# A decoder layer on one core: queries join the ring of six units with keys and values, three buffers go, and the order of all steps is written anew

## What is computed

```python
# attention: 16 heads of 16, causal, only the 32 largest scores of a row kept
scores = einsum('bhqd,bhkd->bhqk', q, k) / sqrt(16), causal
attn   = softmax(top-32 of each row of scores, the rest -inf)
y      = (attn @ v) @ Wo.T + bo
x = layernorm(x + y)
# experts: all 8 computed for every token, gated by sums over a context
h = relu(einsum('edi,bsi->bsed', proj_in, x))        # hidden 512
o = einsum('eid,bsed->bsei', proj_out, h)
x = layernorm(x + einsum('bsei,bse->bsi', o, gate))
# feed-forward: Hadamard, 4-bit activations, ternary weights
x = layernorm(x + quantised(x @ H) @ ternary(W).T)
```

## Time and profile before

| what | value |
|---|---|
| median of 3 runs | 575.65 us (575.60 to 576.58) |
| span of the profiled execution | 574.0 us |
| its own time | not listed apart from its span; the median lies 1.65 us above the span |
| TensorE busy | 521.3 us, 91% |
| VectorE busy | 457.4 us, 80% |
| ScalarE busy | 409.2 us, 71% |
| GpSimd busy | 346.6 us, 60% |

### The profile page before, as it was taken

How to read it: one execution, slowest core, us unless ns; L and a number is a source line. 1 busy time by engine, 2 the same in 40 slices (tenths; PEclk the granted TensorE clock), 3 DMA queues, 4 the chain that set the end, 5 groups by cost and what they waited for, 6 DMA issues and landing times. The chain is left out here.

```text
span 574.0 us, 22290 instructions
## 1 busy us (share of the span) xinstructions
PE 521.3 (91%) x8116; PEld 443.4 (77%) x8116; DVE 457.4 (80%) x2846; ACT 409.2 (71%) x1018; POOL 346.6 (60%) x355
## 2 busy tenths in 40 slices
PE   5757659999999999999999999999999999999973
PEld 3535548888888888888888888888888888888851
DVE  2698988896988989998998889998999899504115
ACT  2888788776767687768866687768686878566641
POOL 1587485955547466755574556656565756476762
PEclk9888888999999999999999999999999999999995
DMA  7544440002000101100120102000200010000000
GB/s 228 174 150 148 126 157 18 3 2 59 3 24 18 23 3 38 40 3 21 41 58 2 23 11 67 3 22 3 76 4 22 2 39 3 1 2 19 2 14 24
DMA packets 23230, 24.08 MB, mean 42 GB/s; under 512 B 2129, under 2 KB 20049, under 8 KB 23121
## 3 DMA queue, kind: packets, MB, share of 16 engines
q1 hardware_dynamic: 23120, 22.65, 13.0%
HBM read 18.32 MB, written 2.10 MB: 36 GB/s over the span
## 5 line engine op out<-in xcount | busy, mean ns | idle before, releaser
L541 POOL TENSOR_TENSOR h_lo<-h_raw,h_hi 128x512 f16<-128x512 f32 x128 | 148.9, 1164 | 114.4 <-ACT h_raw L693 113.0
L895 PE MATMUL ps_o<-w_hi,h_lo 128*128 128x256 f16 x512 | 139.7, 273 | 3.5 <-POOL h_lo L541 3.5
L879 PE MATMUL ps_z<-x1t_hi,w_lo 128*128 128x256 f16 x512 | 140.0, 273 | 0.2 <-DVE x1t_lo L1043 0.2
L879 PE MATMUL ps_z<-x1t_lo,w_hi 128*128 128x256 f16 x512 | 139.7, 273 | 0.0
L879 PE MATMUL ps_z<-x1t_hi,w_hi 128*128 128x256 f16 x512 | 139.6, 273 | 0.0
L895 PE MATMUL ps_o<-w_hi,h_hi 128*128 128x256 f16 x512 | 139.6, 273 | 0.0
L895 PE MATMUL ps_o<-w_lo,h_hi 128*128 128x256 f16 x512 | 139.5, 273 | 0.0
L689 ACT ACTIVATE h_hi<-ps_z 128x512 f16<-128x512 f32 x128 | 76.2, 595 | 71.7 <-PE ps_z L879 71.6
L987 DVE MATCH_REPLACE8 taken<-next,taken 128x64 f32<-128x64 f32 (+4 forms) x480 | 110.7, 242 | 0.1
L562 POOL TENSOR_TENSOR acc<-go_sb,acc 128x512 f32<-128x512 f32 x55 | 70.0, 1273 | 34.3 <-ACT go_sb L703 34.2
L982 DVE MAX8 next<-taken 128x8 f32<-128x64 f32 (+4 forms) x480 | 85.5, 245 | 0.1
(11 more groups left out here) (142 smaller groups left out, 1037.3 us busy)
## 6 DMA issues: line engine op xcount, KB each, us to landing
w_raw<-in_w1t SPq DMA_DIRECT2D x8, 512.0 KB, 3.8
w_raw<-in_w2t SPq DMA_DIRECT2D x8, 512.0 KB, 3.7
v_pad<-v_sb SPq DMA_DIRECT2D x16, 136.0 KB, 2.7
xt_sb<-in_xt SPq DMA_DIRECT2D x8, 256.0 KB, 3.9
x_sb<-in_x SPq DMA_DIRECT2D x8, 256.0 KB, 3.1
xa_sb<-in_xt SPq DMA_DIRECT2D x7, 256.0 KB, 3.7
out<-out_sb SPq DMA_DIRECT2D x7, 256.0 KB, 3.8
ctx_sb<-in_ctx_w SPq DMA_DIRECT2D x8, 128.0 KB, 3.2
```

What stands on the lines that cost most here:

```text
L541: nc.gpsimd.tensor_tensor(h_lo[:, e % 2, 2 * z:2 * z + 2, :], h_raw[:, z, :, :], h_hi[:, e % 2, 2 * z:2 * z + 2, :], ALU.subtract)\
L879: last = pe.matmul(ps_z[z][:, d * UT:(d + 1) * UT], w[:, e, c, at:at + P], x[:, c, :], start=n == 0, stop=n == len(terms) - 1)
L895: last = pe.matmul(ps_o[e % 2][:, b * D:(b + 1) * D], h[:, e % 2, c, b * SEQ:(b + 1) * SEQ], w[:, e, c, :], start=n == 0, stop=n == len(te ...
```

## The change

Queries get a ring of six units like the keys; one transfer into `xa_sb` serves q, k and v of a unit, and it waits for all three of the unit before. `xt_sb`, `x_sb`, `t1` and `out_sb` go: x is loaded into `xb_sb` and gets the bias there, the first LayerNorm works in `x1`, the third in `t3`, which is also what the store reads. New waits keep these shared buffers safe. The tables of slots are replaced by one written list of step names for each engine (`ORDER`); which unit or tile a name means follows from its count.

```diff
-STEADY = {
-    "move_v": 0.75, "shift0": 0.75, "shift1": 0.25, "shift2": 0.5, "shift3": -1.25, "scores": -6.75,
...
+ORDER = {
+    "pe": """
+        q k ffn_sum v scores*2 w_sum*2 v scores turn_probs k q turn_probs w_sum scores attend turn_probs k
...
-        xt_sb, xa_sb = sb("xt_sb", [P, CD, UT]), sb("xa_sb", [P, CD, UT])
-        qt_sb = sb("qt_sb", [P, GROUPS, UT])
+        xa_sb = sb("xa_sb", [P, CD, UT])
+        qt_sb = sb("qt_sb", [P, RING, GROUPS, UT])
...
-        had_sb, ffn_sb = out_sb, x2
+        had_sb, ffn_sb = t3, x2
...
-                elif name == "load_xa":
-                    wait(sp, k_ready, v if v > 1 else 0)
-                    wait(sp, v_ready, v if v > 1 else 0)
+                if name == "load_xa":
+                    for done in (q_ready, k_ready, v_ready):
+                        wait(sp, done, v)
...
-                    wait(sp, xb_ready, v)
-                    sp.dma_start(x_sb[:, :, :], x.rearrange("b s d -> s b d")[:, v * UB:(v + 1) * UB, :])\
+                    wait(sp, t1_ready, v)
+                    sp.dma_start(xb_sb[:, :, :], x.rearrange("b s d -> s b d")[:, v * UB:(v + 1) * UB, :])\
...
                 elif name == "ffn_residual":
                     pool.wait_ge(f_scaled, v + 1)
-                    wait(pool, out_ready, OUTS[v][0])
+                    pool.wait_ge(s_store, 16 * (v + 1))
...
                     act.wait_ge(q_ready, v + 1)
-                    wait(act, spread_ready, TILES * v)
+                    wait(act, spread_ready, TILES * (v - RING + 1))
...
                 elif name == "ln1_apply":
-                    wait(act, x1t_ready, v)
-                    wait(act, acc_done, EXPERTS * (v - 1) + 1)
-                    layernorm_apply(0, x1, t1, v, x1_ready)
+                    layernorm_apply(0, x1, x1, v, x1_ready)
                 elif name == "ln3_apply":
-                    act.wait_ge(s_store, 16 * (v + 1))
-                    layernorm_apply(2, out_sb, t3, v, out_ready)
+                    layernorm_apply(2, t3, t3, v, out_ready)
...
                     act.wait_ge(ready, v + 1)
+                    if name == "x1t_high":
+                        wait(act, l1_done, RING_STEPS * v)
...
-                    wait(dve, x1_ready, v)
-                    V.tensor_tensor(t1[:, :, :], ps_misc[:, :].rearrange("p (b n) -> p b n", b=UB),
+                    wait(dve, x1t_ready, v)
+                    wait(dve, acc_done, EXPERTS * (v - 1) + 1)
+                    V.tensor_tensor(x1[:, :, :], ps_misc[:, :].rearrange("p (b n) -> p b n", b=UB),
```

More of the change, by code:

```diff
@@ L105, in expert_steps @@
     return steps + [("L2", EXPERTS - 1, 0), ("L2", EXPERTS - 1, 1)]
-SLOTS = 4 * EXPERTS
-FINISH = SLOTS + 1
-STEADY = {
-    "move_v": 0.75, "shift0": 0.75, "shift1": 0.25, "shift2": 0.5, "shift3": -1.25, "scores": -6.75,
[L113 to L147, removed]
[3 rows of a table removed]
-    "gated_add": 2.5, "quantise": 85.5, "load_x": -14.5, "gate_scale": 48.75, "store": 102.75, "move_v": 10.25,
-    "q": -11.5, "load_ctx": 29.75, "gate_out": 0.5, "x1t_low": 43.75,
-}
@@ L155 @@
-FINAL = STEADY | {
-    "hadamard": 86.75, "copy_q4t": 99, "ffn": 130.5, "ffn_residual": 97.5, "ffn_scale": 97.25, "turn_q4": 99.75,
-    "to_q4": 86.75, "gate_out": -15, "quantise": 87.5, "out_proj": 59, "move_v": -4.25, "v": 98.5, "gate_sums": 31.5,
-    "turn_o": 38.25, "x2t_high": 80.25, "experts": 51.25, "keep": 4.5, "copy_probs": 2.5, "copy_q": -12,
-    "load_x": -18.25, "copy_k": -13, "rstd3": 97.5, "x1t_high": 52.25, "rstd2": 79, "load_xt": -25.25, "shift1": 2,
-    "turn_x1": 44, "x2t_low": 82.75, "normalise": 6.5, "x_plus_bo": 22, "x1t_low": 53.25, "shift0": 10, "attend": 5,
-    "gate_scale": 59, "h_low": -2.5, "turn_probs": 0.25, "turn_x2": 81.75, "select": 8, "spread_q": -11.75,
-    "copy_probs2": 4, "load_ctx": 26.5, "k": 75.25, "shift2": 2, "gated_add": 4, "copy_scores": -8.25, "relu": -2,
-    "pace": 1.25, "q": -9, "copy_v": 121.25, "scores": -5.5, "store": 105, "ln2_apply": 81.5, "shift3": 0.75,
-    "ln1_stats": 38, "rstd1": 39.5, "ln1_apply": 38.5, "turn_probs2": 8.25, "copy_ot": 36.75,
-}
@@ L220, in build_schedule, with all_steps @@
+def all_steps():
+    for v in range(UNITS):
+        for kind, e, z in expert_steps():
+            yield "pe", kind, v, e, z
+            if kind == "L1":
+                yield "act", "relu", v, e, z
+                yield "pool", "h_low", v, e, z
+            elif z == 1 and not (v == SPLIT and e == EXPERTS - 1):
+                yield "act", "gate_out", v, e
+                yield "pool", "gated_add", v, e
         for k in range(TILES):
-            tile = base + SLOTS // TILES * k + at[f"shift{k}"]
@@ L230, in build_schedule @@
[L230 removed]
+                yield engine, name, v, k
+            for half in range(2):
+                yield "pe", "turn_probs", v, k, half
+                yield "act", "copy_probs", v, k, half
         for b in range(UB):
[L232 removed]
+            yield "dve", "gate_sums", v, b
+            if v == SPLIT:
+                yield "dve", "gated_last", v, b
         for engine, name in UNIT_STEPS:
[L234 to L235 removed]
+            yield engine, name, v
@@ new lines, in build_schedule @@
+def build_schedule():
+    waiting = {}
+    for engine, name, v, *args in all_steps():
+        waiting.setdefault((engine, name), []).append((v, args))
+    waiting = {key: iter(sorted(steps)) for key, steps in waiting.items()}
+    placed = []
+    for engine, words in ORDER.items():
+        for word in words.split():
+            name, _, count = word.partition("*")
+            for _ in range(int(count or 1)):
+                v, args = next(waiting[engine, name])
+                placed.append((engine, name, v, args))
+    return placed
```

218 lines of the change are left out of this document (137 added, 81 removed), and 3 rows, old and new, of the table LAST.

## The result

The changed kernel takes 569.46 us (median of 4, 567.45 to 570.21), the kernel before beside it 575.64 (4 runs, 575.60 to 576.58): a ratio of 0.9893 with a 95% interval of 0.9867 to 0.9918, 6.2 us less. The profiled execution took 568.73, its span 566.9 (before 574.0).

A forecast was written before the change was run, and what follows sets the result against it. VectorE was taken to set the start, TensorE's own work the middle. Span 574.0 + 4.0 (start) - 5.5 (gaps) = 572.5; with 1.65 to the median 574.15, shaded by 0.3 to 573.9 us; own range 572 to 576, overall 569.5 to 579.5.

The forecast's parts named there:

- What bounds the kernel: Whole kernel: VectorE sets the start, TensorE's own work the middle; order can only fill the start, begin experts earlier, close gaps.
- VectorE's first tile at 20.6: Start: VectorE's first attention tile begins at 20.6 us, 2.6 later than before, since ternary sum and values precede the scores.
- 73.2 us of VectorE work to `x1t_low`: Start: VectorE's listed work from its first tile through `x1t_low` of unit 0 takes 73.2 us, ending at 93.8 without waits.
- Rival (1): Start: VectorE's list waits as before, 5.4 us, all ahead of `x1t_low`; slower, 579.3 us; chance 0.20.
- Behind it: Start, after `x1t_low`: TensorE still does the values of unit 4 before the first expert step, taken as 2.8 us.
- the first L1 was forecast for 96.6: End of the start: first expert step begins at 93.8 + 2.8 = 96.6 us, 7.9 later than 88.67.
- 3.9 us of work already done: Start: TensorE does 3.9 us more work before the first L1, so of 7.9 us lateness only 4.0 is lost.
- 5.5 of 7.9 us of gaps: Middle: closes 5.5 of 7.9 us TensorE idle: `h_lo` 2.7, queries behind Hadamard steps 1.1, `turn_o` 0.7, `p_sb` 1.0.
- The rest at nothing: Transfers, LayerNorm waits, `ffn_residual` and `x1t_high` cost nothing; the end keeps its steps, moving 0.2 us at most.
- Rival (2): Start loses less (values at 1.97, unit 4's values at 1.97), other 2.4 us of middle gaps close: 569.5 us; chance 0.17.

The follow-up runs named there:

- run 6: The changed kernel unaltered, a third time, on the chip of run 10 and run 11: 569.89 us, ratio 0.9897 to the kernel before.
- run 7: Kernel before with the new in-place buffers alone, queries out of the ring, old order: 575.33 us beside 575.56, ratio 0.9996.
- run 1: Changed kernel's buffers and single x transfer with the old order on every engine, queries early: 589.44 us, ratio 1.0254 to the kernel before.
- run 11: Changed kernel's order without the query ring (one buffer, own x transfer; queries of units 3 to 5 later): 572.34 us, ratio 0.9938 to the kernel before.
- run 8: Changed kernel with L1/L2 pairs taken apart in five units, on TensorE's list alone: 581.29 us, ratio 1.0104 to the kernel before.
- run 2: Kernel before with six L1/L2 swaps on TensorE, against waits for `h_lo`: 573.33 us beside 574.79, ratio 0.9973.
- run 10: Changed kernel with first scores between ternary sum and values, and ScalarE's values copy behind the weight squares: 569.32 us, ratio 0.9887 to the kernel before.
- run 5: The changed kernel again, same file: 568.75 us, ratio 0.9885 to the kernel before.
- run 12: run 10 plus one L1 piece between scores and attention product in unit 1: 568.56 us, ratio 0.9891 to the kernel before.
- run 4: Changed kernel with the values of unit 4 behind the first L1 piece instead of ahead: 570.61 us, ratio 0.9919 to the kernel before.

## Why the prediction was off, step by step

**What bounds the kernel** was right: VectorE's list sets most of the start, TensorE's own work the middle, and the gain is work moved ahead and gaps closed.

**VectorE's first tile at 20.6** was wrong: 17.25, 18.84 and 17.12 in three executions. The second projection was taken to end at 14.15 and the values to take 3.21, both as in the one profile of before. The values took 1.99 each time, and the second projection 1.99 in two of the three. That slowness was the clock of an execution, not a property of the step.

**73.2 us of VectorE work to `x1t_low`** has nearly the measured length, 73.75 (17.25 to 91.00 and 18.84 to 92.59), but by luck: in the first execution VectorE was busy for 71.1 of it and idle for 2.6, of which 1.3 was one wait for the output projection. So the work was taken 2 us too long, and the waits at nothing. Rival (1) with 5.4 us of waits did not come. **Behind it** 2.8 was taken for the values of unit 4; from the end of `x1t_low` to the first L1 it was 4.1 and 3.8. In these two executions `x1t_low` did not hold up the values. TensorE went without a gap from `turn_x1` (88.21, released by a `normalise` of VectorE) through scores, a weight sum and half a turn to the values, all at the lower clock (0.50 from 88.2 to 94.9), and these began 0.8 behind `x1t_low`; in run 6 they began right behind it. The errors partly cancel: the first L1 was forecast for 96.6 and came at 95.08, 96.43 and 93.73. The Trainium skill's page "TensorE: Matmul & The Clock Gate", section "Why this matters for your kernels", asks only that longer idle gaps be avoided; by it the prediction estimated 1.97 for this projection. The rows show 3.46.

**3.9 us of work already done** was right: 3.58 of own time.

**5.5 of 7.9 us of gaps** is the step that failed, and in its size, not its mechanism. The gaps closed as named (`h_lo`, `quantise`, `turn_o`, `p_sb`), and the idle column gave 5.88. But the sum took the idle column for what the gaps cost. They cost 11.77 in 24 places, not 7.9, and 8.79 went, not 5.5: 0.16 us for each wait that closed is booked as busy. To this come 1.25 us of changes between kinds of matmul, which the forecast left out. On the profiled spans, against the 572.5 of the forecast's sum: 3.3 from the waits, 1.25 from the changes, 1.5 from the earlier first L1, less 0.3 of work and 0.1 of the end, is 5.6, and 572.5 - 566.9 is 5.6.

**What closed them.** Not the buffers (run 7: 0.2 us, within noise). Not the early queries alone (run 1: they cost 14 us in the old order). The new order does, with or without the ring (run 11). That it is TensorE's list alone is excluded by run 8, and run 2 shows that taking out only the waits for `h_lo` gives back half at the next step. Which of the moves on VectorE, ScalarE and GpSimd closed the waits for `p_sb` and `quantise` was not separated and stays open.

**The rest at nothing** held: no wait of TensorE for a transfer, a LayerNorm or a late weight is left in the middle beyond 0.4 us.

**Rival (2)**, 569.5, has the measured number, but mostly by other terms: its first term came (the values at 1.99), but the projection of unit 4 was not fast, and of the last 2.4 us of shown gaps only 0.4 closed.

## What to carry to other kernels

Price a gap of TensorE from the start of one step to the start of the next, less what that step takes undisturbed elsewhere; the idle column leaves out the overlap of matmuls (here 0.16 us of each wait, a third of a wait of 0.5). Do not take a duration from the first 20 us of one profile as a property of the step: look at the granted clock there, and at a second execution. Look at what queues behind early work in the engines' lists: here three projections put early cost 14 us in the old order, while in the new one the single one that was tried was worth about 2.

## What the runs showed of the hardware

- The granted clock rose at 9.6 us in one execution of the changed kernel and at 14.1 in another, with the same steps ahead of it, at times within 0.2 us. The runs of the new order scatter by 2.0 to 5.4 us between executions. In run 10 the scatter goes with the clock: 566.4 and 566.6 us at a mean granted clock of 0.965 and 0.963, 568.2 at 0.955, 570.4 to 570.7 at 0.951. In runs 5 and 11 it does not, so the clock is not shown to be all of it.
- Scores and an attention product back to back, 136 matmuls in 1.6 us, were followed in the middle of the product by a stall of 1.4 to 2.0 us behind nothing that the profile names; in run 6 one packet of instructions (0.02 MB) arrived in that time. A piece of 12 matmuls in 1.31 us between the two made the stall vanish (run 12).
- In runs 4, 8 and 11, behind stalls of 1.97, 2.13 and 1.98 us in the full middle, the granted clock was at 1.2 GHz for 3.4 us, and two steps took another 1.8. Behind the 1.97 of run 6 and two others of run 8 (2.09 and 2.04) it stayed at 2.4 GHz.
